# A new order of the work inside each step of a two-layer adapter kernel

## The chip, the core and the metric

The kernel runs on one core of a Trainium2 chip. Its time is the device time of one launch in microseconds (us); for the kernel before it is the median of three runs. The engines of the core are TensorE (PE in the rows, its weight loads PEld), VectorE (DVE), ScalarE (ACT), GpSimd (POOL) and SyncE (SP), whose queue issues nearly all the DMAs. Every engine works through its own list of instructions in order, and semaphores tie the lists together.

## What is computed

x is 64 sequences of 64 tokens with 1,024 features. Two layers follow each other. Each passes x through a rank-16 adapter chosen for the sequence, and the result through a dense 1,024 x 1,024 matrix with four rank-8 experts that a softmax gate mixes; the sum is added to x:

```
def cond(x, A, B, ids):                  # A, B: one pair for each adapter
    Bx = einsum('bni,bri->bnr', x, B[ids])
    return einsum('bnr,bor->bno', Bx, A[ids])
def ffn(c, W, b, A, Bm, Wr):             # 4 experts of rank 8
    y = einsum('bsi,oi->bso', c, W) + b
    gates = softmax(einsum('bsi,ei->bse', c, Wr))
    z = einsum('bsi,eri->bser', c, A)
    return y + einsum('bse,bseo->bso', 2 * gates, einsum('bser,eor->bseo', z, Bm))
x = x + ffn0(cond(x, A0, B0, id0))       # layer 0: router bias and prior too
x = x + ffn1(cond(x, A1, B1, id1))       # layer 1
```

## The kernel before

Everything is rank 16 between the layers, so the kernel never forms the dense product with x. It carries coefficients (`cm`, split into `cf`) of 16 numbers a token and layer, and multiplies the small adapter matrices into the dense ones once per step. Data lie with features across the 128 partitions. A step is 8 sequences (512 tokens); there are 8 steps, g = 0 to 7, and x of a step is 2 MB. Precision is kept by splitting each float32 operand into a high and a low part: ScalarE rounds the high part (`copy`, line 574), VectorE or GpSimd subtracts it to get the low part (`low`, lines 740 and 952), and TensorE adds three products of the parts (lines 307 to 309).

TensorE does the following in step g. "Wide" is the product of the layer-1 adapters `a1s` with the dense matrix `w1s`, 24 matmuls for each of its three parts, in three banks `ps_d`.

- the matmuls of `hr` with `bst` into `ps_h`, then part 0 of wide (`wide(0)`)
- two transposes of `hsb` into `ps_t`, the gate product of layer 0, `route(0)`, into `ps_z`
- `wide(1)` and half of `wide(2)`, then `ht` with `pick` into `ps_h`
- the first `turn`: four transposes of `lp`, the gated expert coefficients of layer 0, which VectorE's softmax writes (line 898)
- the other half of `wide(2)`, then the layer-1 coefficients `query` into `ps_s` (last matmul line 495)
- `project(g + 1, 0)`: the adapters `bst` with the first half of the next step's tokens into `ps_p`, in four chunks, each of which needs `xs_hi` from ScalarE and `xs_lo` from GpSimd
- `route(1)` into `ps_z`; it needs the low part of the layer-1 coefficients (`cf`, line 740) and of `f1s`
- `project(g + 1, 1)`, whose `xs_lo` VectorE writes, the second `turn`, and the results `ps_d`, which VectorE adds into `xraw` (line 942)

In the last step there is no next step to project, and five of the eight result tiles start before the second `turn`.

ScalarE's list has, in order: the four parts of the next step's `bst` (`split_b`), the high part of wide part 0 (`wide_high(0)`, `res`), `ht` and `he`, two chunks of the next x (`split_x`), the exponential of the first softmax (line 686), `wide_high(1)`, `htx`, the coefficients `ce_hi`, the other chunks of x, `wide_high(2)`, the layer-1 coefficients. A chunk of x waits for its DMA. VectorE's list runs alongside: `split_b`, `wide_low(0)`, `ht`, the first softmax, `wide_low(1)`, `ce_lo`, four operations on the query (lines 916 and 919), two `cf`, three chunks of `xs_lo`, the second softmax with the fourth chunk inside it, `wide_low(2)`. GpSimd has four `xs_lo` and one `a1s_lo` in a step.

SP's queue in step g waits for GpSimd's `a1s_lo`, issues 16 gathers of adapters for step g + 2 (lines 251 and 253), then stores four quarters of the result (line 282), each when VectorE has written it. Behind a store that has landed it loads x of step g + 2 into the same place (line 234). The x that ScalarE splits in step g was so loaded behind the stores of step g - 1.

Of the kernel before, what the change touches and what calls it, by code (L numbers as in the profile page):

```python
# [29 lines left out]
P = 128  # L30
D = 1024
KT = D // P
# [3 lines left out]
GROUP = 8  # L36
# [8 lines left out]
LR = EXP * ER  # L45
FC = EXP * (ER + 1)
HC = P + LR + 2
CH = 4
# [19 lines left out]
def two_layer_adapter_lora(nc, x_in, id0_row, all_ids, a0, b0_tab, ab1_tab, w0, w1, exp0, exp0_rows,  # L68
                           exp1_in, exp1_rows, bias, identity, marks, out):
    with ExitStack() as ctx:  # L70
# [161 lines left out]
        def _(sp):  # L232
# [41 lines left out]
            def body(g, par, last):  # L274
                ahead = not (isinstance(g, int) and g >= STEPS - 2)
                if ahead:
                    picks = pick(g + 2)
                    sp.wait_ge(a_lo, g + 2)
                    gather(picks, range(GROUP))
                for i in range(CH - 1 if last else CH):  # L280
                    sp.wait_ge(d_out, KT * g + KC * (i + 1))
                    sp.dma_start(out[bass.ds(g, 1), :, KC * i:KC * (i + 1), :]
                                 .rearrange("a p k t -> p (a k) t"),
                                 xraw[par][:, KC * i:KC * (i + 1), :]).then_inc(stored[i], 16)
                    if ahead and i > 0:
                        sp.wait_ge(stored[i - 1], 16 * g + 16)
                        load_x(g + 2, par, i - 1)
                if ahead:
                    sp.wait_ge(stored[CH - 1], 16 * g + 16)
                    load_x(g + 2, par, CH - 1)  # L290
# [12 lines left out]
        def _(pe):  # L303
# [110 lines left out]
            def body(g, par, last):  # L414
# [34 lines left out]
                if first:  # L449
                    pe.wait_ge(f0x_ready, 2)  # L450
                    for k in range(KT):
                        pe.wait_ge(w1_lo, k + 1)
                        for n in range(2):
                            mm = wide_product(n, a1s, w1s, k)
                            if k == KT - 1:
                                mm.then_inc(m1_done, 1)
                        if k in (3, 4):
                            pick_m0(k - 3, (ps_s, ps_z)[k - 3])
                else:
                    after_step(pe, d_out, KT * g)  # L460
                    wide(0)

# [19 lines left out]
                turn()  # L482
                wide(2, range(KT // 2, 3 * KT // 4 if last else KT))

# [13 lines left out]
                query()  # L498
                if last:
                    wide(2, range(3 * KT // 4, KT))  # L500
                if first:
# [23 lines left out]
                if last:  # L525
                    start_results((0, 1, 2, 3, 4))
                else:
                    project(g + 1, 1)
                pe.wait_ge(l_done, 2 * g + 2)
                turn()  # L530
                if last:
                    from_layers(5)
                    from_layers(6)
# [38 lines left out]
        def _(act):  # L572
# [89 lines left out]
            def body(g, par, last):  # L662
                first = isinstance(g, int) and g == 0
                if not last and not first:
                    act.wait_ge(h_done, g + 1)
                    split_b(g + 1)

                def wide_high(n):
# [18 lines left out]

                wide_high(0)
# [3 lines left out]
                if not last and not first:  # L692
                    split_x(g + 1, 1 - par, 0, [0, 1])
                softmax_exp(0)
                wide_high(1)
                act.wait_ge(htx_done, g + 1)
# [3 lines left out]
                coef_high(0)  # L700
                if first:
                    split_b(g + 1, QUARTERS[0:2])
                if not last:
                    split_x(g + 1, 1 - par, 0, range(CH) if first else [2, 3])
                wide_high(2)
                if first:
                    split_b(g + 1, QUARTERS[2:4])
                if not last:
                    split_x(g + 1, 1 - par, 1, [0])
                act.wait_ge(c1_done, 2 * g + 1)  # L710
# [5 lines left out]
                if first:  # L716
                    m0x_high(0, 2, ps_h)
                if not last:
                    split_x(g + 1, 1 - par, 1, range(1, CH))
                softmax_exp(1)  # L720
# [17 lines left out]
        def _(dve):  # L738
# [102 lines left out]
            def body(g, par, last):  # L841
                first = isinstance(g, int) and g == 0
                if not first:
                    c0_low(g)
                    h_to_sbuf(g)
                if not last and not first:
                    split_b(g + 1)

                def wide_low(n):
# [15 lines left out]
                def softmax(layer):  # L865
# [8 lines left out]
                    if layer == 0:  # L874
# [7 lines left out]
                                      mx.rearrange("p (j a) -> p j a", a=1).to_broadcast([P, TT, EXP]),  # L882
                                      ALU.subtract).then_inc(sm_step, 1)
                    if layer == 1 and not last:
                        split_second_x(g + 1, 1 - par, [3])
# [14 lines left out]
                                      .to_broadcast([P, TT, EXP, ER]), ALU.mult).then_inc(l_done, 1)  # L900

                wide_low(0)
                dve.wait_ge(ht_hi, 2 * g + 2)
                low(ht[:, 1, :], ps_t[:, 0:P], ht[:, 0, :])
                low(he[ELO, :], ps_t[0:LR, P:2 * P], he[0:LR, :]).then_inc(ht_lo, 1)
                softmax(0)
                wide_low(1)
                coef_low(0)
                if first:
                    split_b(g + 1, (0, 1))  # L910

# [8 lines left out]
                for half in range(2):  # L920
                    cols = slice(half * HALF, (half + 1) * HALF)
                    dve.wait_ge(c1_hi, 2 * g + half + 1)
                    low(cf[L1ROWS[half], 1, cols], cm[L1ROWS[half], cols], cf[L1ROWS[half], 0, cols]
                        ).then_inc(c1_lo, 1)
                if first:
                    split_b(g + 1, (2, 3))
# [129 lines left out]
```

## Time and profile before

| | us |
|---|---|
| median of 3 runs | 335.08 (334.63 to 335.91) |
| the profiled execution | 334.41 |
| its span, first to last instruction | 332.7 |
| PE busy | 307.0 (92%) |
| DVE busy | 220.1 (66%) |
| ACT busy | 186.4 (56%) |
| POOL busy | 63.3 (19%) |

In the rows of a stretch stand its start and end, its length, and then, for each engine, busy time and (x) instructions. The granted TensorE clock was 0.995 of full speed over the span. Before 40.37 us the weights and the first x are loaded and split; then come the eight steps. TensorE's busy share is high, but a row's busy time of matmuls is modelled at its end, so the waits are better read from when each instruction starts.

### The profile page before, as it was taken

The numbers are of one execution on the slowest core, as the hardware profiler recorded it, in microseconds if no ns is written. First come the engines' busy times: TensorE is split into PE (matmuls) and PEld (weight loads), VectorE is DVE, ScalarE is ACT, GpSimd is POOL, SyncE is SP. The second block draws the span as 40 slices with busy tenths as digits, with TensorE's granted clock in tenths as the row PEclk, the third lists the DMA queues.
The fourth block names the chain that finished last, engine by engine and source line by source line (L and its number), as shares of the span: only waits on it lengthen the run. The fifth ranks groups of instructions, "written<-read, shape, count | busy, mean of one in ns | idle before, by whom it ended". The sixth has DMA issues, their size and how long they took to land.

```text
span 332.7 us, 6476 instructions
## 1 busy us (share of the span) xinstructions
PE 307.0 (92%) x2048; PEld 284.4 (85%) x2048; DVE 220.1 (66%) x476; ACT 186.4 (56%) x384; POOL 63.3 (19%) x58
## 2 busy tenths in 40 slices
PE   5994998799989998999979999999999999999894
PEld 4453998589978998999979999999999999899783
DVE  2156887686738766686658666777668676864556
ACT  1446976946546565755466465646575657461520
POOL 5600000620042103320143003320332024200000
PEclk9999899999999999999999999999999999999999
DMA  7999973006870388126840587037811783041006
GB/s 267 345 365 381 347 208 156 0 8 167 300 224 0 104 243 302 51 60 212 286 139 0 158 284 250 2 103 244 299 47 55 255 292 92 0 193 62 1 0 252
DMA packets 30773, 56.16 MB, mean 169 GB/s; under 512 B 3633, under 2 KB 20050, under 8 KB 30754
## 3 DMA queue, kind: packets, MB, share of 16 engines
q1 hardware_dynamic: 29666, 52.97, 48.3%
q0 software_dynamic: 1088, 2.97, 2.5%
q8 instruction: 8, 0.13, 0.1%
q14 instruction: 11, 0.09, 0.1%
HBM read 39.15 MB, written 16.78 MB: 168 GB/s over the span
## 4 chain that ended last, share of the span: by engine, by line
issue 41%; PE 20%; DMA 13%; POOL 12%; DVE 6%; ACT 3%; SPq 2%; POOLq 1%; DVEq 0%; ACTq 0%
POOL xs_lo L952 8%; DMA out<-xraw 6%; DMA xraw<-x_in 6%; PE ps_d L307 3%; PE ps_d L309 3%; PE ps_d L308 3%; POOL a1s_lo L952 2%; DVE xs_lo L740 2%; DVE xraw L942 2%; PE ps_d L545 1%; PE ps_p L307 1%; PE ps_d L547 1%; ACT res L574 1%; SPq L253 1%; SPq L251 1%
## 5 line engine op out<-in xcount | busy, mean ns | idle before, releaser
L952 POOL TENSOR_TENSOR xs_lo<-xraw,xs_hi 128x512 fp32r<-128x512 f32 x28 | 36.0, 1290 | 182.5 <-ACT xs_hi L574 182.4
L307 PE MATMUL ps_d<-w1s_hi,a1s_hi 128*128 128x384 f32 (+1 forms) x192 | 63.9, 333 | 0.0
L309 PE MATMUL ps_d<-w1s_hi,a1s_lo 128*128 128x384 f32 (+1 forms) x192 | 62.0, 323 | 0.0
L308 PE MATMUL ps_d<-w1s_lo,a1s_hi 128*128 128x384 f32 (+1 forms) x192 | 61.9, 322 | 0.0
L942 DVE SCALAR_TENSOR_TENSOR xraw<-ps_d,lp,xraw 128x512 f32<-128x512 f32 x60 | 43.6, 748 | 22.5 <-PE ps_d L547 22.5
L574 ACT ACTIVATE xs_hi<-xraw 128x512 fp32r<-128x512 f32 x60 | 36.0, 626 | 26.4 <-DMA xraw<-x_in 25.9
L307 PE MATMUL ps_p<-xs_hi,bst_hi 128*128 128x256 f32 x120 | 36.5, 304 | 6.2 <-DVE bst_lo L740 2.4
L308 PEld LDWEIGHTS ps_d<-w1s_lo,a1s_hi 128*128 128x128 f32 x192 | 36.2, 189 | 0.0
L307 PEld LDWEIGHTS ps_d<-w1s_hi,a1s_hi 128*128 128x128 f32 x192 | 36.1, 188 | 0.0
L309 PEld LDWEIGHTS ps_d<-w1s_hi,a1s_lo 128*128 128x128 f32 x192 | 36.1, 188 | 0.0
L308 PE MATMUL ps_p<-xs_lo,bst_hi 128*128 128x256 f32 x120 | 34.5, 288 | 0.0
L309 PE MATMUL ps_p<-xs_hi,bst_lo 128*128 128x256 f32 x120 | 34.4, 287 | 0.0
L307 PE MATMUL ps_d<-cf,res 128*128 128x256 f32 x120 | 34.4, 286 | 0.0
L309 PE MATMUL ps_d<-cf,res 128*128 128x256 f32 x120 | 33.9, 282 | 0.0
L308 PE MATMUL ps_d<-cf,res 128*128 128x256 f32 x120 | 33.8, 281 | 0.0
L740 DVE TENSOR_TENSOR res<-ps_d,res 64x384 fp32r<-64x384 f32 (+1 forms) x48 | 24.3, 507 | 12.8 <-ACT res L574 12.3
L574 ACT ACTIVATE res<-ps_d 64x384 fp32r<-64x384 f32 (+1 forms) x48 | 21.3, 443 | 18.3 <-PE ps_d L309 17.9
L307 PEld LDWEIGHTS ps_p<-xs_hi,bst_hi 128*128 128x128 f32 x120 | 23.5, 196 | 9.4 <-DVE bst_lo L740 3.3
L952 POOL TENSOR_TENSOR a1s_lo<-abraw,a1s_hi 128x1024 fp32r<-128x1024 f32 x7 | 17.0, 2431 | 39.5 <-ACT a1s_hi L574 39.5
L545 PE MATMUL ps_d<-ce_hi,erows 128*128 128x512 f32 x60 | 24.3, 405 | 0.0
L308 PEld LDWEIGHTS ps_p<-xs_lo,bst_hi 128*128 128x128 f32 x120 | 23.6, 197 | 0.3
L547 PE MATMUL ps_d<-ce_lo,erows 128*128 128x512 f32 x60 | 23.7, 395 | 0.0
(227 smaller groups left out, 702.9 us busy)
## 6 DMA issues: line engine op xcount, KB each, us to landing
out<-xraw SPq DMA_DIRECT2D x31, 512.0 KB, 3.5
xraw<-x_in SPq DMA_DIRECT2D x28, 512.0 KB, 5.0
w_plain<-w SPq DMA_DIRECT2D x16, 512.0 KB, 8.9
abraw<-ab_tab SPq DMA_DIRECT2D x64, 128.0 KB, 2.1
b0raw<-b_tab SPq DMA_DIRECT2D x64, 64.0 KB, 2.0
xraw<-x_in POOLq DMA_DIRECT2D x4, 512.0 KB, 11.0
a_plain<-a SPq DMA_DIRECT2D x1, 512.0 KB, 3.6
out<-xraw SPq DMA_DIRECT2D x2, 256.0 KB, 2.7
```

The source lines that it names most:

```text
L251: sp.dma_start(b0raw[:, b, :], b0_tab[bass.ds(n0, 1)].rearrange("a p n -> p (a n)")).then_inc(signal, 16)
L253: sp.dma_start(abraw[:, b, :, :].rearrange("p a n -> p (a n)"), ab1_tab[bass.ds(n1, 1)].rearrange("a p n -> p (a n)")).then_inc(signal, 16)
L307: pe.matmul(acc, lh, rh, start=first, stop=False, skip_group_check=True)
L308: pe.matmul(acc, lh, rl, start=False, stop=False, skip_group_check=True)
L309: return pe.matmul(acc, ll, rh, start=False, stop=final, skip_group_check=True)
L545: pe.matmul(acc[:], erows[:, m * P:(m + 1) * P], ce_hi[:], start=False, stop=False, skip_group_check=True)
L547: pe.matmul(acc[:], erows[:, m * P:(m + 1) * P], ce_lo[:], start=False, stop=True, skip_group_check=True).then_inc(d_done, 1)
L574: return act.activation(dst, src, ACT.Copy)
L740: return dve.tensor_tensor(dst, whole, high.bitcast(F32), ALU.subtract)
L942: dve.scalar_tensor_tensor(out=xraw[par][:, m, :], in0=banks[m % len(banks)][:], scalar=bsum[:, m:m + 1], in1=xraw[par][:, m, :], op0=ALU. ...
L952: return pool.tensor_tensor(dst, whole, high.bitcast(F32), ALU.subtract)
```

## The change

No operation is added or removed in the steps; their places move. TensorE computes three of the eight chunks of `wide(0)` before the transposes of `hsb`, and the other five and a quarter of `wide(1)` after `route(0)`. The rest of `wide(1)` follows the first `turn`, and all of `wide(2)` follows the query. ScalarE and VectorE do the exponential and the coefficients of layer 0 first, and all of `split_b` and the wide parts afterwards; ScalarE splits all four chunks of the next x in a row. SP's gathers are dealt out between the four stores, and a load now follows two stores later instead of one. Step 0 keeps TensorE's order, and the last step starts four result tiles instead of five before its second `turn`.

```
 SP     if ahead:  sp.wait_ge(a_lo, g + 2)
-           gather(picks, range(GROUP))
 for i in range(CH - 1 if last else CH):
+    if ahead:
+        gather(picks, (range(0, 3), range(3, 5), range(5, 7), range(7, 8))[i])
     (store i)
-    if ahead and i > 0:  wait stored[i - 1]; load_x(g + 2, par, i - 1)
+    if ahead and i > 1:  wait stored[i - 2]; load_x(g + 2, par, i - 2)
 PE     after_step(pe, d_out, KT * g)
-       wide(0)
+       wide(0, range(3))
        route(0, f0x)
-       if not first:
-           wide(1)
-       wide(2, range(KT // 2))
+       if first: wide(2, range(KT // 2))
+       else:     wide(0, range(3, KT)); wide(1, range(2))
        turn()
-       wide(2, range(KT // 2, 3 * KT // 4 if last else KT))
+       if first: wide(2, range(KT // 2, KT))
+       else:     wide(1, range(2, KT))
        query()
-       if last:  wide(2, range(3 * KT // 4, KT))
+       if not first:  wide(2)
        if last:
-           start_results((0, 1, 2, 3, 4))
+           start_results((0, 1, 2, 3))
```

The diff of ScalarE and VectorE only moves calls, and the lists below show them. They are the loop's steps. The names are the tiles written and read, as in the text above; `bst_lo` are the four low parts of `split_b`, and `res<-ps_d` with 384 columns is `wide_low(0)`.

VectorE before, from the first softmax's last row to the layer-1 coefficients:

```order
L898 TENSOR_TENSOR lp<-hsb,lg 128x4x32
L854 REGISTER_ALU
L740 TENSOR_TENSOR f1s<-ps_d,f1s 64x36
L740 TENSOR_TENSOR res<-ps_d,res 64x256
L854 REGISTER_ALU
L740 TENSOR_TENSOR f1s<-ps_d,f1s 64x36
L740 TENSOR_TENSOR res<-ps_d,res 64x256
L862 ISA
L740 TENSOR_TENSOR ce_lo<-ps_t,ce_hi 64x512
L916 SCALAR_TENSOR_TENSOR ps_s<-ps_s,hsb,same_seq 128x256
L919 TENSOR_TENSOR cm<-cm,ps_s 128x256
```

VectorE after, from the last of the four `bst_lo`, which now stand behind `ce_lo`:

```order
L740 TENSOR_TENSOR bst_lo<-abraw,bst_hi 128x4x8x16
L851 ISA
L740 TENSOR_TENSOR res<-ps_d,res 64x384
L851 REGISTER_ALU
L740 TENSOR_TENSOR res<-ps_d,res 64x384
L913 SCALAR_TENSOR_TENSOR ps_s<-ps_s,hsb,same_seq 128x256
L916 TENSOR_TENSOR cm<-cm,ps_s 128x256
L913 SCALAR_TENSOR_TENSOR ps_s<-ps_s,hsb,same_seq 128x256
L916 TENSOR_TENSOR cm<-cm,ps_s 128x256
L740 TENSOR_TENSOR cf<-cm,cf 64x256 x2
L851 REGISTER_ALU
L740 TENSOR_TENSOR f1s<-ps_d,f1s 64x36
```

The splits of `bst` and `wide_low(0)` moved in between `ce_lo` and the query, and `f1s` with the rest of `wide_low(1)` moved behind the two `cf`.

ScalarE before, from `he` to the first coefficients:

```order
L574 ACTIVATE he<-ps_t 32x128
L579 REGISTER_ALU
L580 ISA
L574 ACTIVATE xs_hi<-xraw 128x512
L580 REGISTER_ALU
L574 ACTIVATE xs_hi<-xraw 128x512
L685 ISA
L686 ACTIVATE lg<-lg 128x16
L671 REGISTER_ALU
L574 ACTIVATE f1s<-ps_d 64x36
```

ScalarE after, from the same instruction:

```order
L582 ACTIVATE he<-ps_t 32x128
L689 ISA
L690 ACTIVATE lg<-lg 128x16
L582 ACTIVATE htx<-ps_h 64x256 x2
L683 ISA
L582 ACTIVATE ce_hi<-ps_t 64x512
L685 ISA
L582 ACTIVATE ce_hi<-ce_hi 64x512
L675 ISA
L582 ACTIVATE res<-ps_d 64x384 x2
L594 REGISTER_ALU
L582 ACTIVATE bst_hi<-abraw 128x4x8x16
```

No split of x stands ahead of the exponential (`lg<-lg`) any more; `wide_high(0)` and `bst_hi` follow the coefficients, and the four `xs_hi` come behind them.

TensorE before, at the first `turn`:

```order
L478 MATMUL ps_h<-ht,pick 128x128 x2
L481 REGISTER_ALU
L445 MATMUL ps_t<-ident,lp 128x128 x4
L307 MATMUL ps_d<-w1s_hi,a1s_hi 128x384
L308 MATMUL ps_d<-w1s_lo,a1s_hi 128x384
```

TensorE after, at the same place:

```order
L483 MATMUL ps_h<-ht,pick 128x128 x2
L486 REGISTER_ALU
L448 MATMUL ps_t<-ident,lp 128x128 x4
L310 MATMUL ps_d<-w1s_hi,a1s_hi 128x292
L311 MATMUL ps_d<-w1s_lo,a1s_hi 128x292
```

Behind the `turn` stood twelve 384-column matmuls of part 2; now eighteen 292-column matmuls of part 1 stand there, and the 24 of part 2 behind the query.

## Rows read from the trace of the kernel before

**Rows 1.** Busy time by stretch: step 0, steps 1 to 6, step 6

```profile
40.37:81.33 40.96, 37.20 (x256) 34.70 (x255) 30.81 (x62) 27.69 (x55) 7.51 (x5) 1.00 0.36 107
81.33:297.82 216.49, 209.88 (x1479) 201.62 (x1477) 151.03 (x331) 127.71 (x271) 45.49 (x30) 1.00 0.50 162
262.80:297.82 35.02, 34.81 (x249) 33.59 (x247) 25.37 (x56) 21.28 (x46) 7.62 (x5) 1.00 0.48 167
```

**Rows 2.** TensorE's waits over the span: total us, times, longest us

```profile
PE ps_t L445 <- DVE lp L898: 6.2, 6, 1.7
```

**Rows 3.** Timeline (start, us, instruction, [idle <-releaser]), step 3, first exponential

```profile
166.92 0.63 ACT L574 ACTIVATE xs_hi<-xraw 128x512 fp32r<-128x512 f32 x1 [2.62 <-DMA xraw<-x_in]
...
167.63 1.26 POOL L952 TENSOR_TENSOR xs_lo<-xraw,xs_hi 128x512 fp32r<-128x512 f32 x1 [1.96 <-ACT xs_hi L574]
...
167.69 0.17 DVE L887 TENSOR_REDUCE rs<-lg 128x4 f32<-128x16 f32 x1 [3.25 <-ACT lg L686]
...
168.10 0.82 DVE L891 SCALAR_TENSOR_TENSOR lg<-lg,rs 128x16 f32<-128x16 f32 x1
```

**Rows 4.** Timeline of TensorE, step 3: wide parts 0, 1 and 2

```profile
156.62 0.38 PE L307 MATMUL ps_d<-w1s_hi,a1s_hi 128*128 128x384 f32 x1
...
160.83 0.27 PE L468 MATMUL ps_t<-ident,hsb 128*128 128x128 f32 x1
...
161.86 0.38 PE L307 MATMUL ps_d<-w1s_hi,a1s_hi 128*128 128x292 f32 x1
...
165.15 0.34 PE L307 MATMUL ps_d<-w1s_hi,a1s_hi 128*128 128x384 f32 x1
```

**Rows 5.** Timeline, step 6: VectorE's `bst_lo`, `wide_low(0)` and `wide_low(1)`

```profile
266.70 1.29 DVE L740 TENSOR_TENSOR bst_lo<-b0raw,bst_hi 128x512 fp32r<-128x512 f32 x2
...
269.77 1.14 DVE L740 TENSOR_TENSOR res<-ps_d,res 64x384 fp32r<-64x384 f32 x2 [1.18 <-ACT res L574]
...
275.56 0.18 DVE L740 TENSOR_TENSOR f1s<-ps_d,f1s 64x36 fp32r<-64x36 f32 x1
...
276.22 0.42 DVE L740 TENSOR_TENSOR res<-ps_d,res 64x256 fp32r<-64x256 f32 x1
```

**Rows 6.** Timeline, step 6, from the first `turn` to the second

```profile
275.70 0.66 PE L445 MATMUL ps_t<-ident,lp 128*128 128x128 f32 x4
...
277.78 0.63 ACT L574 ACTIVATE xs_hi<-xraw 128x512 fp32r<-128x512 f32 x1
...
279.68 0.98 ACT L574 ACTIVATE res<-ps_d 64x384 fp32r<-64x384 f32 x2
279.68 0.49 DVE L916 SCALAR_TENSOR_TENSOR ps_s<-ps_s,hsb,same_seq 128x256 f32<-128x256 f32 x1 [1.87 <-PE ps_s L495]
...
281.07 0.42 DVE L919 TENSOR_TENSOR cm<-cm,ps_s 128x256 f32<-128x256 f32 x1
...
281.65 0.87 DVE L740 TENSOR_TENSOR cf<-cm,cf 64x256 fp32r<-64x256 f32 x2 [0.16 <-ACT cf L574]
...
284.36 0.45 DVE L869 TENSOR_REDUCE hsb<-ps_z 128x144 f32<-128x288 f32 x1
...
286.74 0.66 PE L445 MATMUL ps_t<-ident,lp 128*128 128x128 f32 x4
```

**Rows 7.** Timeline, step 0: four chunks of x on ACT and POOL

```profile
57.80 2.17 ACT L574 ACTIVATE xs_hi<-xraw 128x512 fp32r<-128x512 f32 x4
...
58.50 5.08 POOL L952 TENSOR_TENSOR xs_lo<-xraw,xs_hi 128x512 fp32r<-128x512 f32 x4 [44.59 <-ACT xs_hi L574]
...
62.89 1.41 DVE L740 TENSOR_TENSOR cf<-cm,cf 64x256 fp32r<-64x256 f32 x2 [2.34 <-ACT cf L574]
```

**Rows 8.** Timeline of SP's queue, step 3: store and load issues

```profile
155.38 0.96 SPq L282 DMA_DIRECT2D out<-xraw  x2
...
164.94 3.63 SPq L234 DMA_DIRECT2D xraw<-x_in  x2
```

**Rows 9.** Timeline of TensorE, last step: the start of `route(1)`

```profile
316.78 0.27 PE L314 MATMUL ps_z<-f1s,cf 128*128 128x72 f32 x1 [2.07 <-DVE cf L740]
```

More of the change, by code:

```diff
@@ L284, in body @@
                                  xraw[par][:, KC * i:KC * (i + 1), :]).then_inc(stored[i], 16)
-                    if ahead and i > 0:
-                        sp.wait_ge(stored[i - 1], 16 * g + 16)
-                        load_x(g + 2, par, i - 1)
+                    if ahead and i > 1:
+                        sp.wait_ge(stored[i - 2], 16 * g + 16)
+                        load_x(g + 2, par, i - 2)
                 if ahead:
-                    sp.wait_ge(stored[CH - 1], 16 * g + 16)
-                    load_x(g + 2, par, CH - 1)
+                    for i in (CH - 2, CH - 1):
+                        sp.wait_ge(stored[i], 16 * g + 16)
+                        load_x(g + 2, par, i)
                 if last:
@@ L472, in body @@
                 route(0, f0x)
-                if not first:
-                    wide(1)
-                wide(2, range(KT // 2))
+                if first:
+                    wide(2, range(KT // 2))
+                else:
+                    wide(0, range(3, KT))
+                    wide(1, range(2))
                 pe.wait_ge(ht_lo, g + 1)
@@ L482, in body @@
                 turn()
-                wide(2, range(KT // 2, 3 * KT // 4 if last else KT))
+                if first:
+                    wide(2, range(KT // 2, KT))
+                else:
+                    wide(1, range(2, KT))
                 def query():
@@ L498, in body @@
                 query()
-                if last:
-                    wide(2, range(3 * KT // 4, KT))
+                if not first:
+                    wide(2)
                 if first:
@@ L531, in body @@
                 if last:
-                    from_layers(5)
-                    from_layers(6)
+                    for m in (4, 5, 6):
+                        from_layers(m)
                 else:
@@ L700, in body @@
                 coef_high(0)
-                if first:
-                    split_b(g + 1, QUARTERS[0:2])
+                wide_high(0)
                 if not last:
[L704 to L707, printed above, removed]
+                    split_b(g + 1, QUARTERS[0:2] if first else QUARTERS)
                 if not last:
-                    split_x(g + 1, 1 - par, 1, [0])
+                    split_x(g + 1, 1 - par, 0)
+                wide_high(1)
                 act.wait_ge(c1_done, 2 * g + 1)
@@ L717, in body @@
                     m0x_high(0, 2, ps_h)
+                wide_high(2)
+                if first:
+                    split_b(g + 1, QUARTERS[2:4])
                 if not last:
-                    split_x(g + 1, 1 - par, 1, range(1, CH))
+                    split_x(g + 1, 1 - par, 1)
                 softmax_exp(1)
@@ L845, in body @@
                     h_to_sbuf(g)
-                if not last and not first:
-                    split_b(g + 1)
                 def wide_low(n):
@@ L883, in softmax @@
                                       ALU.subtract).then_inc(sm_step, 1)
+                    if layer == 0:
+                        dve.wait_ge(ht_hi, 2 * g + 2)
+                        low(ht[:, 1, :], ps_t[:, 0:P], ht[:, 0, :])
+                        low(he[ELO, :], ps_t[0:LR, P:2 * P], he[0:LR, :]).then_inc(ht_lo, 1)
                     if layer == 1 and not last:
@@ L900, in softmax @@
                                       .to_broadcast([P, TT, EXP, ER]), ALU.mult).then_inc(l_done, 1)
+                softmax(0)
+                coef_low(0)
+                if not last:
+                    split_b(g + 1, (0, 1) if first else range(4))
                 wide_low(0)
[L903 to L910, printed above, removed]
                 dve.wait_ge(q_done, g + 1)
@@ L924, in body @@
                         ).then_inc(c1_lo, 1)
+                wide_low(1)
                 if first:
```

7 lines of the change are left out of this document (removed).

## The prediction, on record before the changed kernel ran

> **What bounds the kernel now.** I read three views in this order. First the busy time by stretch: the steps 1 to 6 take 216.49 us together, the fastest of them 35.02 us with TensorE busy 34.81, and step 0 takes 40.96 [rows 1]. So a step without waits is about 35 us of matmuls, and the change can win only what steps 1 to 5 take above it, 216.49 - 6 x 35.02 = 6.4 us, and waits in step 0 and the last step. Then TensorE's waits: 6.2 us in six places are the first `turn`, which waits for `lp`, the end of VectorE's first softmax [rows 2]. Third the timeline there, to see why the softmax is late. In step 3 VectorE waited 3.25 us for the exponential, and ScalarE had that behind a chunk of x for which it waited 2.62 us [rows 3]. The chunk came late because SP's queue first issued all 16 gathers, let the first store go at 155.38, and reached the last two loads at 164.94 and 168.2 [rows 8]. A second loss sits in the same rows: a VectorE operation on 16 elements, both inputs in SBUF, took 0.82 us from 168.10 to 168.92, while GpSimd worked on `xs_lo` until 168.89.
>
> I time one step from three marks: S, its first matmul on `hr`; T, the first `turn`; U, the second. In step 6, which had no wait at T, S is 262.80 [rows 1], T is 275.70 = S + 12.90, U is 286.74 = T + 11.04 [rows 6], and the next S is 297.82 = U + 11.08.
>
> **TensorE's new order, S to T.** 18 matmuls of 292 columns and 12 of 384 move behind T. The pace of part 0 is (160.83 - 156.62) / 24 = 0.175 us a matmul, that of part 1 (165.15 - 161.86) / 24 = 0.137 [rows 4]. So 18 x 0.137 + 12 x 0.175 = 2.47 + 2.10 = 4.57 us move, and TensorE can be at T at S + 8.33. VectorE must deliver `lp` by then. `route(0)` ends at about S + 4.8: the old start of the transposes less 15 matmuls of 384 columns, plus its own 1.03 us (161.86 - 160.83). The softmax behind it takes 2.32 us (second softmax to second `turn`, 286.74 - 284.36, which holds 0.69 us of one x chunk as the first now holds 0.6 of `ht` and `he`) to 2.6 us. `lp` is there at S + 7.4, 0.9 us early. No x stands ahead of the exponential now, and GpSimd is idle then, so both causes of the wait are gone: **the wait at the first `turn` goes in every step.** If its cover fails, each 0.1 us late costs 0.6 us in all.
>
> **x and the gathers.** ScalarE now comes to x at T + 5.2 (below), S + 13.5. With the gathers dealt out, the stores no longer stand behind 16 gathers at about 0.5 us each; the first goes some 5 us earlier and the last loads about as much. In step 3 the last x load issued near 168.2, the end of the pair in [rows 8], which is S + 13.6; five us earlier, plus its landing time, it is there by S + 14, and ScalarE wants that fourth chunk at S + 15. I cost x and the gathers at nothing; the cover is about 1 us.
>
> **T to U, where the price is.** The same 4.57 us of matmuls now lie here, so T to U would be 11.04 + 4.57 = 15.61 if nothing else changed. I follow each engine from T.
>
> - ScalarE is free of `ce_hi` at 277.78 = T + 2.08 [rows 6]. `wide_high(0)` takes 1.00 (279.68 to 280.68), four `bst_hi` of 128 x 512 take 0.53 each, the pace of four x chunks in [rows 7]. x starts at T + 5.20 and ends at T + 7.3; `wide_high(1)` ends at T + 8.25.
> - GpSimd starts 0.70 us after ScalarE's first chunk and needs 5.08 us for four [rows 7]: T + 5.90 to T + 10.98.
> - TensorE ends the query at T + 4.16 and all of `wide(2)` (24 x 0.175 = 4.21) at T + 8.37. `project` wants its fourth chunk at T + 10.5 and gets it at T + 11.03: 0.5 us of wait. `route(1)` could start at T + 11.75.
> - VectorE starts `bst_lo` 0.67 us after ScalarE's first, T + 3.75. Four take 4 x 0.60 and `wide_low(0)` 1.17 with the gap behind it [rows 5], the four query operations 1.72 (279.68 to 281.07 and the pace behind) [rows 6]. The two `cf` can start at T + 9.05. Before, VectorE waited 1.87 us for the query; now it is 3.0 us late for it. Then two `cf` 0.90, `wide_low(1)` 1.03 (275.56 to 276.64) [rows 5], three `xs_lo` 1.81 (284.36 less 281.65 less 0.90) and 2.38 from softmax to `turn` [rows 6]. Without any holding, the chain and the short waits for ScalarE in it come to U = T + 15.47.
>
> So VectorE's list, not TensorE's, now sets U, and there is no slack left in it. And the two `cf` lie inside GpSimd's run. In step 0 they did so before: a pair that takes 0.87 us alone [rows 6] took 1.41 from 62.89, released about 0.15 us before GpSimd's end at 63.58 [rows 7]. The operation at 168.10 was released at the same point [rows 3]. So the first `cf` is held from T + 9.05 to the end of GpSimd's third chunk, T + 9.71 - 0.15 = T + 9.56, and the second, by then behind the fourth, to T + 10.83. It ends at T + 11.26 instead of T + 9.95 or so. Everything behind it on VectorE follows: `wide_low(1)` to T + 12.25, `xs_lo` to T + 14.05, U = T + 16.45. **The price is 1.0 us a step**; TensorE waits for it at `route(1)`, in `project(g + 1, 1)` and at the second `turn`.
>
> The Trainium skill, SBUF — State Buffer, section "Who interferes with whom", says that a VectorE instruction with two SBUF inputs contends with a GpSimd instruction that reads SBUF, and that whoever comes first holds the pair for its whole instruction while the other fully blocks. The traces agree in those two rows, and by that rule the sum is the one I give; without it, it would be the first rival's.
>
> **The sum.** A step 1 to 6: 8.33 + 16.45 + 11.08 = 35.86, six are 215.2, **-1.3** against 216.49. Step 0: `lp` comes 0.55 us earlier, but `wide_high(0)` now stands before its x, so GpSimd starts 1.0 us later, and `wide_high(2)`, two `bst_hi` and `wide_low(1)` before the second half of x; the second `turn` comes from VectorE's list at 70.8 instead of 69.7: **+1.1**. The last step has no GpSimd work. `route(1)` waited 2.07 us [rows 9]; now 24 matmuls, 4.2 us, cover the coefficients instead of 6, and they are ready 0.5 us before. Against that the second `turn` follows four tiles instead of five and waits 0.3 us: **-2.1**. The sum is -2.3 us. The profiled execution, 334.41, becomes 332.1; it lay 0.67 us under the median of 335.08, so the median becomes **332.8**.
>
> **Rivals.**
> 1. VectorE isn't held, or the two `cf` fall between two GpSimd chunks. For it: not every operation is held, since the reduction at 167.69, with one input, took 0.17 us beside the same GpSimd chunk [rows 3]. Against: both operations of two SBUF inputs above. A step is 8.33 + 15.47 + 11.08 = 34.88, six are 209.3, -7.2; with +1.1 and -2.1 that is -8.2, or 326.9.
> 2. GpSimd's next chunk always wins, so the first `cf` waits to T + 10.83 as well. No row shows an operation of VectorE that waits across two chunks, so I can't exclude it. U = T + 16.87, a step 36.28, six 217.7, +1.2; step 0 +1.4, last -2.1: +0.5, or 335.6.
> 3. On the other side, slower: each holds the other. The fourth `bst_lo` (T + 5.56 to 6.2) pushes GpSimd's start by 0.2 and the first `cf` its fourth chunk by 0.45, so that chunk ends at T + 11.6 and the second `cf` at T + 11.9. U = T + 17.1, a step 36.5, six 219.1, +2.6; step 0 +1.5, last -2.1: +2.0, or 337.1. It decides once GpSimd's chunks there take 1.45 us instead of the 1.27 of [rows 7].
> 4. The change doesn't do what it says: gathers between the stores delay the stores that follow, and x is late at T + 5.2 too. Each us of it falls on GpSimd's chain and so on U: above 338. The 1 us of cover speaks against it.
>
> **How the numbers follow.** My forecast gets 0.40, rival 1 0.17, rival 2 0.25, rival 3 0.13, rival 4 0.05. The lower end goes into rival 1 and the upper to rival 3: 327.3 to 337.2. About 0.5% (1.7 us) is what a measurement of this kernel can tell from no change. Faster by more, under 333.4: rival 1 and two thirds of the forecast, 0.43. Within it, to 336.8: the rest of the forecast and most of rival 2, 0.36. Slower: 0.21.
>
> **What would show it.** In the profile after: no wait of `ps_t` for `lp` at the first `turn`, which comes near S + 8.3; ScalarE without a wait for x; GpSimd's four chunks back to back; a `cf` pair of 1.5 to 2.3 us instead of 0.87; new waits of TensorE for `f1s` or `cf` at `route(1)` and for `xs_lo` or `lp` behind; U near T + 16.4. The last step should show no wait at `route(1)`. A `cf` pair of 0.9 us would prove my main term wrong, and steps of 37 us or waits of ScalarE for x would prove rival 3 or 4 right.

## The result: slower by 0.8%, not faster by 0.7%

| | before | after |
|---|---|---|
| median of 14 runs each | 334.91 us (331.99 to 339.33) | 337.34 us (335.25 to 339.42) |
| ratio, with its 95% interval | | 1.0079 (1.0053 to 1.0105) |
| the profiled execution | 334.41 | 336.79 |
| its span | 332.7 | 335.1 |

Forecast were 332.8 us and a range up to 337.2; the median lies 0.1 us above its upper end, in the time of rival 3 (337.1). From the profile page of after, the engines' busy time and the largest group of GpSimd:

```profile
PE 310.5 (93%) x2048; PEld 285.7 (85%) x2048; DVE 223.7 (67%) x476; ACT 186.6 (56%) x384; POOL 65.2 (19%) x58
...
L950 POOL TENSOR_TENSOR xs_lo<-xraw,xs_hi 128x512 fp32r<-128x512 f32 x28 | 37.9, 1382 | 183.8 <-ACT xs_hi L582 183.8
```

GpSimd does what it did, but a chunk now takes 1.38 us in the mean, where four took 5.08 together in [rows 7]. The busy time by stretch of after, in the columns of [rows 1]: step 0, steps 1 to 6, the last step, and two us in the second half of step 0:

```profile
38.68:83.09 44.41, 40.05 (x256) 37.51 (x255) 32.64 (x63) 29.38 (x57) 7.64 (x5) 0.92 0.41 130
83.09:302.57 219.48, 212.78 (x1478) 201.94 (x1477) 154.24 (x331) 127.59 (x271) 47.23 (x30) 1.00 0.47 155
...
302.57:335.10 32.53, 27.67 (x190) 26.34 (x188) 18.73 (x45) 9.43 (x23) 0.00 (x0) 1.00 0.21 85
...
66.00:68.00 2.00, 1.54 (x7) 1.57 (x8) 1.97 (x4) 0.51 (x1) 0.00 (x0) 0.50 0.00 0
```

The span grew by 2.4 us. Against [rows 1] the stretch before step 0 is 1.69 us shorter (38.68 for 40.37), since TensorE's clock fell to 0.50 in it before and not after; step 0 is 3.45 longer (44.41 for 40.96), steps 1 to 6 are 2.99 longer (219.48 for 216.49), and the last step is 2.35 shorter (32.53 for 332.7 less 297.82 = 34.88). In step 0 the granted clock stood at 0.50, the lower of its two levels (1.2 GHz of 2.4), from about 65.6 to 72.5 us. The fall begins inside a TensorE wait of 0.96 us for `xs_lo`, which ends at 66.46; the mean of 0.92 over the 44.41 us is a loss the order alone does not make. The kernel with the old queue (second experiment) shows step 0 with this order, the same waits of TensorE to 0.01 us (2.04, 0.44 and 0.96) and a clock of 1.00: 42.84 us. So the order costs 1.9 us there and the clock 1.6, and those waits alone do not decide whether the clock falls. Every profile of this study has such a fall, at varying places; here it moved from one stretch to another, and the two nearly cancel.

The steps 1 to 6 are alike to 0.05 us: T = S + 8.34, U = T + 17.15, next S = U + 11.08, together 36.57. The timeline of step 4, whose S is 192.82: the two marks, ScalarE's x, GpSimd, the end of VectorE's `bst_lo`, and its list from the coefficients on (start, us, instruction, [idle before it <- its releaser]):

```profile
201.16 0.62 PE L448 MATMUL ps_t<-ident,lp 128*128 128x128 f32 x4
...
211.20 0.39 PE L310 MATMUL ps_p<-xs_hi,bst_hi 128*128 128x256 f32 x1 [0.23 <-POOL xs_lo L950]
...
212.61 0.39 PE L310 MATMUL ps_p<-xs_hi,bst_hi 128*128 128x256 f32 x1 [0.44 <-POOL xs_lo L950]
...
213.31 0.28 PE L312 MATMUL ps_p<-xs_hi,bst_lo 128*128 128x256 f32 x1
213.68 0.30 PE L317 MATMUL ps_z<-f1s,cf 128*128 128x72 f32 x1
...
214.48 0.26 PE L319 MATMUL ps_z<-f1s,cf 128*128 128x36 f32 x1
214.84 0.36 PE L310 MATMUL ps_p<-xs_hi,bst_hi 128*128 128x256 f32 x1
...
218.31 0.44 PE L448 MATMUL ps_t<-ident,lp 128*128 128x128 f32 x2
...
199.95 0.29 DVE L899 TENSOR_TENSOR lp<-hsb,lg 128x128 f32<-128x128 f32 x1
...
206.80 0.69 DVE L740 TENSOR_TENSOR bst_lo<-abraw,bst_hi 128x512 fp32r<-128x512 f32 x1
...
209.95 0.42 DVE L916 TENSOR_TENSOR cm<-cm,ps_s 128x256 f32<-128x256 f32 x1
210.29 2.56 DVE L740 TENSOR_TENSOR cf<-cm,cf 64x256 fp32r<-64x256 f32 x2
212.88 0.19 DVE L740 TENSOR_TENSOR f1s<-ps_d,f1s 64x36 fp32r<-64x36 f32 x1
...
213.43 0.20 DVE L740 TENSOR_TENSOR f1s<-ps_d,f1s 64x36 fp32r<-64x36 f32 x1
...
214.00 1.90 DVE L740 TENSOR_TENSOR xs_lo<-xraw,xs_hi 128x512 fp32r<-128x512 f32 x3
215.93 0.46 DVE L866 TENSOR_REDUCE hsb<-ps_z 128x144 f32<-128x288 f32 x1
...
206.43 2.18 ACT L582 ACTIVATE xs_hi<-xraw 128x512 fp32r<-128x512 f32 x4
...
207.12 5.43 POOL L950 TENSOR_TENSOR xs_lo<-xraw,xs_hi 128x512 fp32r<-128x512 f32 x4 [23.16 <-ACT xs_hi L582]
```

The reader should see three things. `lp` is written at 200.24, 0.92 us before the first `turn` at 201.16, which shows no wait. The `cf` pair, 0.87 us in [rows 6], takes 2.56 us, and ends 0.30 us behind GpSimd's 5.43. And TensorE waits for GpSimd's third and fourth chunk, and later for VectorE's `xs_lo` (0.24 us before 217.48). The view marks no wait for `cf` or `f1s`, but the starts show one: matmuls of this kind start 0.11 to 0.12 us apart, and the first of `route(1)` starts 0.37 us behind its forerunner (213.31 to 213.68), right after VectorE's second `f1s` (213.43 to 213.63). That is 0.25 us of wait; the next start, at 214.84, has as much for VectorE's first `xs_lo`.

Single chunks and single `cf` of the same stretch, from the views of those tiles in short windows (count, shortest/median/longest in ns, start):

```profile
L950 POOL TENSOR_TENSOR xs_lo<-xraw,xs_hi x1: 1518/1518/1518, 207.1 to 207.1; 128x512 fp32r<-128x512 f32 x1
...
L950 POOL TENSOR_TENSOR xs_lo<-xraw,xs_hi x1: 1296/1296/1296, 208.6 to 208.6; 128x512 fp32r<-128x512 f32 x1
...
L950 POOL TENSOR_TENSOR xs_lo<-xraw,xs_hi x1: 1285/1285/1285, 209.9 to 209.9; 128x512 fp32r<-128x512 f32 x1
...
L950 POOL TENSOR_TENSOR xs_lo<-xraw,xs_hi x1: 1458/1458/1458, 211.1 to 211.1; 128x512 fp32r<-128x512 f32 x1
...
L740 DVE TENSOR_TENSOR cf<-cm,cf x1: 1126/1126/1126, 210.3 to 210.3; 64x256 fp32r<-64x256 f32 x1
...
L740 DVE TENSOR_TENSOR cf<-cm,cf x1: 1397/1397/1397, 211.4 to 211.4; 64x256 fp32r<-64x256 f32 x1
```

GpSimd's first chunk starts while VectorE's fourth `bst_lo` (206.80 to 207.49) is under way, and takes 1.52 us instead of 1.29: it is held. The first `cf` is ready at 210.29 and held until the third chunk is nearly over; alone it takes 0.42, so it ran from about 211.00 to 211.42. The fourth chunk had to wait for that and took 1.46. The second `cf` waited for the fourth chunk and ended at 212.85. So each engine holds the other in turn. The experiments below bear each half of this out.

### The profile page after: what moved, and what is told of

It is laid out like the page before. It is cut to its first block, busy times and chain, and to the rows that moved or that the text cites. A ratio compares the mean times of both kernels' runs of the same rounds, so it can differ in the third digit from the quotient of the medians.

```text
span 335.1 us, 6476 instructions
## 1 busy us (share of the span) xinstructions
PE 310.5 (93%) x2048; PEld 285.7 (85%) x2048; DVE 223.7 (67%) x476; ACT 186.6 (56%) x384; POOL 65.2 (19%) x58
## 4 chain that ended last, share of the span: by engine, by line
PE 43%; DVE 20%; issue 12%; ACT 9%; DMA 7%; POOL 3%; SPq 3%; POOLq 0%; DVEq 0%; ACTq 0%
PE ps_d L310 8%; PE ps_d L312 7%; PE ps_d L311 7%; DMA xraw<-x_in 5%; DVE xs_lo L740 4%; PE ps_d L555 3%; PE ps_d L553 3%; DVE bst_lo L740 3%; DVE res L740 3%; PE ps_h L317 3%; ACT bst_hi L582 2%; DMA out<-xraw 2%; DVE w1s_lo L740 2%; PE ps_t L448 2%; DVE xraw L940 1%
## 5 line engine op out<-in xcount | busy, mean ns | idle before, releaser
L950 POOL TENSOR_TENSOR xs_lo<-xraw,xs_hi 128x512 fp32r<-128x512 f32 x28 | 37.9, 1382 | 183.8 <-ACT xs_hi L582 183.8
L310 PE MATMUL ps_p<-xs_hi,bst_hi 128*128 128x256 f32 x120 | 37.8, 315 | 12.5 <-POOL xs_lo L950 7.0
L582 ACT ACTIVATE xs_hi<-xraw 128x512 fp32r<-128x512 f32 x60 | 33.8, 620 | 3.9 <-DMA xraw<-x_in 3.0
L740 DVE TENSOR_TENSOR ce_lo<-ps_t,ce_hi 64x512 fp32r<-64x512 f32 x16 | 10.9, 683 | 24.1 <-ACT ce_hi L582 24.1
L740 DVE TENSOR_TENSOR cf<-cm,cf 64x256 fp32r<-64x256 f32 (+1 forms) x24 | 23.5, 980 | 0.7 <-ACT cf L582 0.5
L312 PEld LDWEIGHTS ps_p<-xs_hi,bst_lo 128*128 128x128 f32 x120 | 23.9, 199 | 0.0
```

The source lines that it names most:

```text
L310: pe.matmul(acc, lh, rh, start=first, stop=False, skip_group_check=True)
L312: return pe.matmul(acc, ll, rh, start=False, stop=final, skip_group_check=True)
L582: return act.activation(dst, src, ACT.Copy)
L740: return dve.tensor_tensor(dst, whole, high.bitcast(F32), ALU.subtract)
L950: return pool.tensor_tensor(dst, whole, high.bitcast(F32), ALU.subtract)
```

## The experiments

Each is timed beside the kernel before, on the same chip. Ratios are to that kernel, with the 95% interval. The kernel before took 335.08 us beside the first four, 337.31 (333.75 to 338.14) beside the four on the hold, and 334.86 beside the last two; against 335.08 the ratios of those on the hold would be about 0.007 higher, so the steps in their traces are the safer measure of what they gain. "Step" is one of the steps 1 to 6, S, T and U the marks of the prediction.

### The queue of SyncE alone

Before, with only the new order of gathers, stores and loads:

```
-  gather(picks, range(GROUP))
   for i in range(...):
+      gather(picks, (range(0, 3), range(3, 5), range(5, 7), range(7, 8))[i])
       (store i)
-      if i > 0: wait stored[i - 1]; load_x(g + 2, par, i - 1)
+      if i > 1: wait stored[i - 2]; load_x(g + 2, par, i - 2)
```

> The kernel before with SP's new queue order alone (gathers dealt out between the stores, loads two stores behind). Theory A, of the prediction: x lands about 5 us earlier, ScalarE has no wait for it and the first turn none, so steps 1 to 5 fall to about 35 us and the time to about 329. Theory B, from the profile of the changed kernel, where the first load left only 1.5 us earlier against S than before and the last 2.3 us: the wait for the second chunk of x, which sets the first turn, shrinks by less than 1 us, and the time is within 2 us of before, 333 to 335.

It took 364.28 us, ratio 1.085 (1.074 to 1.097); no theory had this. From its profile page:

```profile
L577 ACT ACTIVATE bst_hi<-abraw 128x512 fp32r<-128x512 f32 x16 | 10.0, 623 | 42.6 <-DMA abraw<-ab_tab 42.6
```

ScalarE waits 42.6 us for the gathers. In the order of before `split_b` stands at the start of a step (S + 2.3 in step 4), some 9 us ahead of where it stands after (S + 11.5 in step 3), and the gathers dealt out between the stores have not landed by then: in step 3 of this trace it starts at S + 9.5, after 7.65 us of wait. So the new queue needs `split_b` moved back. The two parts of the change belong together, which the prediction had not said. Part of the loss is the clock: beside TensorE's waits for `he`, `lp` and `cf` it stood at 0.50 seven times, for 3 to 7 us, and its mean is 0.946 against 0.995 in the profile before. By these means the clock accounts for at most 18 us (364.4 x 0.054 less 332.7 x 0.005) of the 31.7 that the span grew.

> The changed kernel with SP's old queue order (all 16 gathers ahead of the first store). Theory A (SP's order is what lets ScalarE take four chunks of x in a row): the fourth chunk lands at about S + 18.5 and is wanted at S + 15, so each of the six steps is 2 to 3 us longer, 352 or so. Theory B (it matters little): the wait of ScalarE for x grows from 0.6 to at most 1.5 us, steps of 37.2, time 338 to 342.

The other way round, after with the old queue (the same lines, reversed): 340.94 us, ratio 1.020 (1.011 to 1.028). ScalarE waits 12.6 us for x in eleven places. Steps without such a wait are still 36.6 us with U = T + 17.15; in step 3 the pair starts only at T + 11.2, takes 0.87 us, and GpSimd's four chunks take 5.26 instead of 5.44. The two kinds of step stand side by side in this one trace, step 3 with its pair behind the chunks (it starts at 178.01) and step 4 with it among them (214.07):

```profile
172.76 5.26 POOL L947 TENSOR_TENSOR xs_lo<-xraw,xs_hi 128x512 fp32r<-128x512 f32 x4 [23.21 <-ACT xs_hi L579]
...
210.72 5.45 POOL L947 TENSOR_TENSOR xs_lo<-xraw,xs_hi 128x512 fp32r<-128x512 f32 x4 [24.09 <-ACT xs_hi L579]
```

So the fourth chunk's stretch of 0.18 belongs to the pair. The new queue is worth 1.2% here (1.020 against 1.008), some 3.6 us, and the theory of 352 us was far off. Its trace of step 1 alone has 3.4 us of that, 40.03 for 36.6, with x late and a fall of the clock in it.

### The exponential ahead of x, in the kernel before

```
 ScalarE   he
+          softmax_exp(0)
           split_x(g + 1, 1 - par, 0, [0, 1])
-          softmax_exp(0)
```

> The kernel before with one edit: ScalarE does the first exponential ahead of the two chunks of x instead of behind them, nothing else. Theory A (the wait at the first turn is only the exponential behind x, and GpSimd's hold of the next VectorE operation): steps 1 to 6 take 35.0 to 35.1 each, 210.5 together against 216.5, and the time is 329. Theory B (x that is late now holds wide_high(1), htx and the query instead): half of it comes back at the query, steps of 35.6, 332.

336.53 us, ratio 1.001 (0.996 to 1.006): no difference. The wait of [rows 2] at the first `turn` is gone in the steps 1 to 6 (T = S + 12.84 to 12.88, against 13.36 to 14.72 before in steps 1 to 5), and the time does not fall. From the waits of its trace:

```profile
PE ps_p L307 <- POOL xs_lo L952: 5.0, 8, 1.3
```

TensorE waits for `xs_lo` in `project` instead, 5.0 us in all, in steps 1 to 3 most, and U comes up to 14.95 us behind T (11.38 before). x is late there for its own reason: ScalarE waits 15.2 us for it in 14 places. The wait at `turn` had covered the wait for x. But not all of the 14.95 is wait. The profiled execution was one of 338.58 us, and behind the waits of 1.20 and 1.29 us in steps 2 and 3 its clock stood at 0.50 from about 139.8 to 143.0 and from 177.5 to 184:

```profile
175.58 0.39 PE L307 MATMUL ps_p<-xs_hi,bst_hi 128*128 128x256 f32 x1 [1.29 <-POOL xs_lo L952]
...
178.00:183.00 5.00, 5.00 (x25) 5.00 (x24) 3.95 (x12) 1.33 (x3) 2.06 (x1) 0.50 0.00 0
```

Of those 10 us up to 5 are lost to the clock, and step 4, without a wait or a fall, takes 34.78. So the 6.4 us by which I took steps 1 to 5 to be too long were not to be had from the exponential alone; how much of what was lost again is late x, and how much the clock beside it, one trace does not settle.

### Step 0 in the old order

> The changed kernel with ScalarE's and VectorE's old order in step 0 alone. In the profile after, step 0 took 44.4 us against 41.0, and TensorE's granted clock was at half for 6.6 us of it. Theory A (the new order of step 0 makes a longer wait of TensorE there, and the clock falls behind it): step 0 is back at 41 us, the clock at full in it, and the time is 3 us less than the changed kernel's, 334. Theory B (the fall of the clock is the chip's and lies where it will): step 0 loses only the 1.2 us of its order, the clock falls there or elsewhere, and the time is 336.

After, with ScalarE's and VectorE's old lists in step 0: 335.7 us, ratio 1.003 (0.999 to 1.007), some 1.6 us less than after. Its step 0 is 42.03 us with a fall of the clock in it. So the new order of step 0 is a loss of 1.2 to 1.9 us, the lower figure from the last experiment below. Steps 1 and 6 of this trace take 37.54 and 37.53 us for the 36.6 of the others, with a fall of the clock in each, although the waits of TensorE that the views mark ahead of it, about 0.26 and 0.45 us for `xs_lo`, are those of every step.

### The hold, from three sides

First the operands. `low` of the pair reads `cm` and `cf`, both in SBUF. Here the sum stays in PSUM, so that one operand is no longer in SBUF; ScalarE then reads both halves after VectorE has written both:

```
-  tensor_tensor(cm[:, cols], cm[:, cols], ps_s[:, cols], ALU.add)
+  tensor_tensor(ps_s[:, cols], cm[:, cols], ps_s[:, cols], ALU.add)
-  copy(cf[..., 0, cols], cm[...]); low(cf[..., 1, cols], cm[...], cf[..., 0, cols])
+  copy(cf[..., 0, cols], ps_s[...]); low(cf[..., 1, cols], ps_s[...], cf[..., 0, cols])
```

> The changed kernel, with the layer-1 coefficients (cm + ps_s) kept in PSUM, so that the pair of cf on VectorE reads one operand from PSUM and one from SBUF; ScalarE reads both halves only once both are there. Theory A (VectorE is held because both inputs are in SBUF while GpSimd reads SBUF): the pair takes 0.9 us instead of 2.55 and ends at T + 11.0 instead of T + 11.7; the second turn comes at T + 16.4 instead of T + 17.15, a step takes 35.85 instead of 36.57, 4.4 us less in all. Theory B (VectorE's list is late by itself and the pair only absorbs it): the second turn stays at T + 17.1.

332.22 us, ratio 0.987 (0.980 to 0.995). The timeline of its step 4 (T is 198.55, U 214.97):

```profile
208.63 0.88 DVE L738 TENSOR_TENSOR cf<-ps_s,cf 64x256 fp32r<-64x256 f32 x2 [0.85 <-ACT cf L582]
...
204.52 5.27 POOL L948 TENSOR_TENSOR xs_lo<-xraw,xs_hi 128x512 fp32r<-128x512 f32 x4 [23.16 <-ACT xs_hi L582]
```

The pair runs in 0.88 us in the midst of GpSimd's chunks, although ScalarE makes it wait 0.85 us first. GpSimd's four take 5.27: the fourth takes 1.29, the first still 1.53 beside `bst_lo`. U = T + 16.42, a step 35.83: 0.74 us less than after.

Second the cause. GpSimd subtracts only 16 of 256 columns of a chunk's rows and fills the rest of `xs_lo` with zeros, so most of the low part of the first half of each next x is left out of the computation:

```
-  low(xs[1][chunk], xraw[par][chunk], xs[0][chunk])
+  low(xs[1][chunk, 0:16], xraw[par][chunk, 0:16], xs[0][chunk, 0:16])
+  memset(xs[1][chunk, 16:], 0.0)
```

> The changed kernel, with most of the low part of x's first half left out: GpSimd subtracts 16 of 256 columns of each chunk and fills the rest with zeros, so that it writes but hardly reads SBUF. It isn't the whole computation. Theory A (a GpSimd operation that reads SBUF holds VectorE): the cf pair takes 0.9 us and the second turn is at T + 15.5. Theory B (any GpSimd work holds it): the pair starts at T + 9.1 and still takes 1.3 us or more as long as GpSimd is busy.

327.74 us in one run. The pair still has both operands in SBUF and is not held, but by then no GpSimd work is left (the last `memset` ends at T + 8.8, the pair starts at T + 9.15); a step is 35.13. So it gives the price of all that GpSimd does to the step, hold and late chunks together, 1.44 us, but does not tell them apart. It does show the other direction once more. Its first and second small subtraction in step 4:

```profile
202.41 0.48 POOL L950 TENSOR_TENSOR xs_lo<-xraw,xs_hi 128x32 fp32r<-128x32 f32 x1 [23.18 <-ACT xs_hi L582]
...
203.30 0.25 POOL L950 TENSOR_TENSOR xs_lo<-xraw,xs_hi 128x32 fp32r<-128x32 f32 x1
```

The first starts while the fourth `bst_lo` runs (202.10 to 202.78) and takes 0.23 us more, as much as the chunk 16 times its size: what GpSimd loses depends on how much of VectorE's instruction is left, not on the size of its own.

Third the place. VectorE does `wide_low(1)`, which reads `ps_d` in PSUM, ahead of the pair, both as in after:

```
+  wide_low(1)
   for half in range(2): low(cf[..., 1, cols], cm[...], cf[..., 0, cols])
-  wide_low(1)
```

> The changed kernel with wide_low(1) ahead of the cf pair on VectorE; both stay in SBUF. Theory A (wide_low(1), with one input in PSUM, runs under GpSimd's fourth chunk in the time in which the pair was held): wide_low(1) at T + 9.1 to T + 10.2, the pair to T + 12.1, second turn at T + 16.4, steps of 35.85. Theory B (the pair is held as long in its new place): T + 17.1, steps of 36.6.

331.48 us, ratio 0.984 (0.977 to 0.991), a step 35.76, U = T + 16.33. The pair of its step 4, in the view of the tile:

```profile
L740 DVE TENSOR_TENSOR cf<-cm,cf x2: 422/846/1271, 208.8 to 210.1; 64x256 fp32r<-64x256 f32 x2
```

The first `cf` comes at 208.8, just after the fourth chunk began, and is held for 1.27 us; the second runs free in 0.42. GpSimd's four take 5.29: the chunk that came first isn't stretched. A pair that is held once costs 0.85 us, and `wide_low(1)` was done in time that the hold wasted in after.

Both together:

> Both edits: wide_low(1) ahead of the pair, and the pair with its operand in PSUM. Theory A: nothing on VectorE is held, the pair ends at T + 11.0, xs_lo follows at once, and the second turn is at T + 15.6, set by TensorE's own work and GpSimd's fourth chunk: steps of 35.0, 9.5 us less than the changed kernel, 328. Theory B (the granted clock falls further when TensorE waits less): steps without a fall of the clock are 35.0, but the falls take back half of it, 332.

330.13 us, ratio 0.980 (0.973 to 0.987), a step 35.5, U = T + 16.07 where 15.6 was expected. The pair is not held any more (0.88 us), and only the first chunk still is (1.53). Yet TensorE waits 0.25 and 0.27 us for GpSimd's third and fourth chunk, and VectorE 0.49 for ScalarE's second half of x.

### A version that beats both: shorter lists in front of x

On top of the two edits together, and in the steps 1 to 6 alone (the lines are marked against after):

```
 ScalarE  coef_high(0)
-         wide_high(0)
          split_b; split_x(g + 1, 1 - par, 0)
+         wide_high(0)
-         wide_high(1)
          copy cf, both halves
+         wide_high(1)
 VectorE  split_b
-         wide_low(0)
          query operations
+         wide_low(0)
-         wide_low(1)
          low cf, both halves
+         wide_low(1)
```

> Edit, on top of the version with the coefficients in PSUM and wide_low(1) ahead (e7, 330.13 us, step 35.5, U = T + 16.07): in steps 1 to 6 ScalarE goes from the four bst_hi straight to the four chunks of x and does wide_high(0) behind them and wide_high(1) behind the coefficients; VectorE does the query operations ahead of wide_low(0), and then the cf pair ahead of wide_low(1), with cf still read from PSUM. Nothing is left out. Theory A, that with the hold gone GpSimd's start sets U: ScalarE's x comes 1.0 us earlier, GpSimd runs its four chunks from T + 4.96 to about T + 10.25 (still 5.28 us, the first of them 1.5 because the fourth bst_lo runs beside its start), TensorE's two waits for xs_lo in project(g + 1, 0), 0.25 and 0.27 us, go, U = T + 15.55, step 34.97, six steps 3.1 us less than e7, 327.0 us in all (326 to 328). Theory B, that VectorE's list or ScalarE's second half of x sets U whatever GpSimd does: U stays at T + 16.0 and more, 329.5 to 330.5 us.

327.34 us (325.57 to 328.94), ratio 0.977 (0.972 to 0.982). Its stretches of steps 3 and 4, and under them, from the view of ScalarE's `xs_hi` in the steps 1 to 4, what ended its idle time (us, times):

```profile
154.09:189.25 35.16, 34.72 (x248) 33.53 (x247) 24.15 (x56) 21.08 (x46) 7.71 (x5) 1.00 0.51 168
189.25:223.81 34.56, 34.56 (x249) 33.43 (x247) 24.06 (x56) 20.99 (x46) 7.72 (x5) 1.00 0.51 171
```

```profile
  DMA xraw<-x_in: 2.2, 4
```

In steps 4 to 6 U = T + 15.12 and TensorE has no wait: 34.56 us of 34.56 are busy. This is what TensorE's own order needs; my 15.61 for T to U was 0.5 us too long, since the 11.04 of [rows 6] held that much waiting. The starts of TensorE in step 6 of the kernel before show it, in two places where the view marks no wait:

```profile
283.05 0.26 PE L316 MATMUL ps_z<-f1s,cf 128*128 128x36 f32 x1
283.39 0.35 PE L307 MATMUL ps_p<-xs_hi,bst_hi 128*128 128x256 f32 x1
...
285.49 0.28 PE L309 MATMUL ps_p<-xs_hi,bst_lo 128*128 128x256 f32 x1
285.91 0.39 PE L307 MATMUL ps_p<-xs_hi,bst_hi 128*128 128x256 f32 x1
```

The starts lie 0.34 and 0.42 us apart where 0.11 and 0.12 is the pace, 0.53 us of wait. So after loses 36.57 - 34.56 = 2.0 us a step to GpSimd and VectorE. In the steps 1 to 3 x is now late: ScalarE waits 2.2 us in four places, and the steps take 35.87, 35.26 and 35.16. The cover of the prediction's second part is used up.

> Edit, on top of the one above (e10): ScalarE and VectorE take the order of the kernel before in step 0, with the coefficients in PSUM there too. Nothing is left out. If the new order in step 0 costs what the comparison of e8 with the changed kernel says (1.2 to 1.6 us), step 0 falls from 42.60 us to 41.0 to 41.4 and the median is 1.2 to 1.6 us under that of e10; with theory A this is 325.6 us (324.5 to 327), some 2.8% under the kernel before. If the loss in step 0 was only the fall of TensorE's clock that happened to lie there, step 0 stays above 42 us in a profile with a clock fall in it and the median is that of e10.

327.43 us, ratio 0.976 (0.972 to 0.980): the same as without it. The stretches of its step 0 and its steps 1 to 4:

```profile
41.73:82.78 41.05, 37.19 (x257) 34.70 (x255) 29.43 (x61) 27.07 (x54) 7.48 (x5) 1.00 0.35 109
...
82.78:224.83 142.05, 139.06 (x987) 134.13 (x985) 96.68 (x221) 84.61 (x181) 30.86 (x20) 1.00 0.50 167
```

Step 0 is 1.15 us shorter (41.05 for 42.20), just under the 1.2 to 1.6 expected, and the steps 1 to 4 are 1.20 us longer (142.05 for 140.85): ScalarE waits 3.1 us for x in six places instead of 2.2 in four. What step 0 gives, the loads take back. I didn't try to start the loads earlier; why they are late in the early steps and no longer in steps 5 and 6 is open. And four runs of each, from 325.57 to 328.94 us, cannot tell 1 us apart.

## Why the prediction was wrong, point by point

Forecast was -2.3 us, and the span grew by 2.4. Of these 4.7 us the steps 1 to 6 make 4.3 and step 0 2.35 (1.6 of it the clock), the last step makes -0.25 and the stretch before step 0 -1.7.

- **S to T.** Right: T - S 8.33 to 8.37 for 8.33, no wait of `ps_t` for `lp` in the steps 1 to 7, `lp` 0.92 us early for 0.9.
- **What that wait was worth.** The first weak step of the argument. The experiment with the exponential shows that without it the kernel before isn't faster, since x is late behind it. In after x is hardly late (next point), so the argument didn't fail through this, but a sum from the row of waits alone would have.
- **x and the gathers.** The conclusion held, the reason not. In step 3 (S 156.26) the first store went at S - 5.5 instead of S + 0.8, 6.3 us earlier for "some 5", but the last load only 2.3 us, at S + 11.3 instead of S + 13.6; it is the last of the three in the load row below, issued 0.33 us before its end. A load still waits for a store to land, and each load now takes longer: by the profile page's DMA issues the median from issue to landing of a load of x went from 5.0 to 6.8 us. The new queue does this: the kernel before with it has 6.9, and after with the old queue 5.1. So the fourth chunk was 0.58 us late and the cover of 1 us was gone. It cost nothing, because the pair was held until after GpSimd anyway: it started at T + 9.59 instead of T + 9.14 and ended at T + 11.69, as in every step. The rows of the timeline of after, step 3, SP's queue and ScalarE:

```profile
150.77 1.73 SPq L284 DMA_DIRECT2D out<-xraw  x1
...
161.52 6.40 SPq L234 DMA_DIRECT2D xraw<-x_in  x3
...
172.10 0.63 ACT L582 ACTIVATE xs_hi<-xraw 128x512 fp32r<-128x512 f32 x1 [0.58 <-DMA xraw<-x_in]
```

- **T to U.** This is the step that failed. The pair was ready at T + 9.14 for 9.05 and held as described; but I had GpSimd's four chunks at 5.08 us from a place where VectorE left them nearly alone [rows 7], and so counted the hold in one direction. With 5.44 us GpSimd ends at T + 11.40 instead of 10.98, the pair at T + 11.69 instead of 11.26: 0.43 us. The two parts are the 0.23 of the fourth `bst_lo` and the 0.17 of the first `cf`, each against the 1.29 of a free chunk of this trace. Rival 3 named both, with 0.2 and 0.45, and had 0.13 as its chance. The list behind the pair took 5.46 us for 5.19: `wide_low(1)` 1.12 for 1.03 and three `xs_lo` 1.93 for 1.81, where I had subtracted busy times without all gaps (my terms 1.03, 1.81 and 2.38 make 5.22, not the 5.19 between my marks). Together 0.70 us a step, 4.2 us in six steps: U = T + 17.15 for 16.45, and +3.0 us for the steps 1 to 6 where -1.3 stood. That rival 3's 337.1 us lies so near the measured 337.34 is partly luck: it had the chunks end 0.2 us too late and shared the list that was 0.27 us too short, and its +1.5 for step 0 knew nothing of the clock.
- **Step 0.** +1.9 for +1.1 by the trace without a fall in it, +3.45 in this one. Its pair took 2.52 us too (1.41 in [rows 7]), and the fall of the clock came on top in this execution. The old order of step 0 gives 1.2 to 1.9 back when the loads are in time.
- **The last step.** -2.35 for -2.1. `route(1)` has no wait, the start of `turn` follows 0.25 us behind the result tiles.
- **The chances.** Rivals 2 and 3 share the end of the story (chunks and pair interleave, and the pair ends with GpSimd), and the profile gave no reason to take the hold for one-sided. A hold seen in two rows says that two engines exclude each other; the chance of the case where both pay should not have been the smaller one.

The Trainium skill, SBUF — State Buffer, section "Who interferes with whom", says that issue order, not the shape of the operation, decides who blocks. The rows above agree, in both directions: a chunk that comes behind a running `bst_lo` takes 1.52 us, and a `cf` that comes behind a chunk takes up to 0.98 us longer than alone. The same page says that one operand in PSUM, or a GpSimd instruction that only writes, doesn't contend; the pair with its sum in PSUM agrees with the first (0.88 us beside GpSimd), and no run here shows the second, since with the zeros filled in the pair came after the last `memset`.

## What to carry to other kernels

When two engines exclude each other, follow both through the overlap, instruction by instruction: the one that waits slips in between two instructions of the other and lengthens that one's chain as well. Moving work behind an early wait moves it into somebody's slack: write down each list from the new start on and look for operations with two SBUF operands that land beside GpSimd. The cure was cheap: an operand left in PSUM, and work with a PSUM operand done while GpSimd runs, took 337.34 us to 332.22 and 331.48, and both to 330.13 (a step from 36.57 us to 35.83, 35.76 and 35.5), where the reordering alone lost 2.4.

## What was not expected of the hardware

- GpSimd's chunks of 128 x 512 are issued back to back, yet a VectorE operation that waits gets in between two of them: `cf` ran in the gap between 211.00 and 211.42, and the chunk behind took 1.46 us instead of 1.29.
- The waiting engine seems to go on 0.15 to 0.2 us before the end that the profile shows of the other's instruction. This is an estimate from durations: `cf` at 211.42 less its 0.42 is 211.00, against about 211.2 for the chunk, and the small subtraction at 202.41 plus 0.23 is 202.64, against 202.78 for `bst_lo`.
- TensorE's granted clock fell to 0.50 in the midst of every profiled run, for 3.4 us in the one before and 6.8 in the one after, beside waits of TensorE but not beside every one: a wait of 2.41 us ends near 33 us in all twelve profiles, and the clock falls there in eight of them. In the 14 runs of after the time goes from 335.25 us at a mean clock of 0.997 to 339.42 at 0.973, more than the whole effect of the change, so one profiled execution has to be read with its clock row beside it.
- Dealing the gathers out between the stores made the landing of a 512 KB load slower, 6.6 to 7.0 us in the nine profiles with the new queue, 5.0 to 5.2 in the three with the old. Why is not shown.
